# A four-stage hybrid block on one core: inverse sums as column-tile products, folds one step sooner, sine products on GpSimd, and first weights of the second attention split ahead

## The reference, cut to what matters

```python
x = x + _L0_attn_a_ref(_layernorm(x), q_a_w, q_b_w, kv_a_w, kv_b_w, o_w)
x = x + _L0_ffn_ref(_layernorm(x), Wg, Wu, Wd, Wr, temperature)
x = x + _L0_attn_b_ref(_layernorm(x), wq, wk, wv, wo)
x = x + _L0_ffn_ref(_layernorm(x), Wg, Wu, Wd, Wr, temperature)
# attention A, per head: softmax(query @ key.T) @ v, then @ o_w.T
attn = jax.nn.softmax(scores.astype(jnp.float32), axis=-1)
out = jnp.einsum('bhqk,bhkd->bhqd', attn, v)
```

## Time and profile before

| what | value |
|---|---|
| median of 3 runs | 1576.9 us |
| lowest and highest run | 1568.78 and 1577.12 us |
| profiled execution, its own time | 1568.78 us |
| its span, first to last instruction | 1567.0 us |
| instructions in the trace | 26377 |
| mean granted clock of TensorE | 0.979 of full speed |

### The profile page before, as it was taken

One profiled execution on the slowest core, in us unless ns is written; L12 is line 12 of the kernel. 1 busy time (PEld: TensorE's weight loads), 2 busy tenths in 40 slices (PEclk: granted clock), 3 DMA queues, 4 the chain that ended last, 5 costly groups with the idle time before them and its releaser, 6 DMA issues. The chain is left out here.

```text
span 1567.0 us, 26377 instructions
## 1 busy us (share of the span) xinstructions
PE 1464.7 (93%) x8888; PEld 1261.7 (81%) x8888; DVE 1174.5 (75%) x2637; ACT 849.3 (54%) x2068; POOL 630.4 (40%) x509
## 2 busy tenths in 40 slices
PE   5599999999699999997999999999999979999998
PEld 4477777777588888885799999999999868888887
DVE  6688898898775555567888888888888777555554
ACT  3688888887333332323767666666666523333332
POOL 2578888886200000004666666666666400000000
PEclk9799999999899999998999999999999989999999
DMA  2055445544400010001322222222231200001001
GB/s 98 17 124 123 109 116 123 117 108 107 123 21 21 21 41 0 1 1 41 88 67 63 68 56 73 61 68 68 43 87 41 61 21 20 21 22 40 0 1 54
DMA packets 47542, 91.52 MB, mean 58 GB/s; under 512 B 5184, under 2 KB 25664, under 8 KB 47424
## 3 DMA queue, kind: packets, MB, share of 16 engines
q1 hardware_dynamic: 47424, 90.01, 22.7%
HBM read 29.18 MB, written 2.10 MB: 20 GB/s over the span
## 5 line engine op out<-in xcount | busy, mean ns | idle before, releaser
L1722 DVE TENSOR_TENSOR f_hidden<-ps,f_silu 128x512 f32<-128x512 f32 x128 | 87.7, 690 | 201.9 <-PE ps L116 201.9
L1612 ACT ACTIVATE f_silu<-ps 128x512 f32<-128x512 f32 x128 | 76.3, 598 | 282.4 <-PE ps L116 282.4
L387 POOL TENSOR_TENSOR ab_swapped<-ab_swapped,const 128x512 f32<-128x512 f32 x124 | 160.2, 1292 | 169.6 <-ACT ab_swapped L382 169.6
L114 PE MATMUL ps<-xh,f_wl 128*128 128x512 f32 x512 | 203.2, 397 | 1.5 <-DVE f_hidden L1722 1.5
L115 PE MATMUL ps<-xl,f_wh 128*128 128x512 f32 x512 | 202.8, 396 | 0.0
L116 PE MATMUL ps<-xh,f_wh 128*128 128x512 f32 x512 | 202.6, 396 | 0.0
L1438 POOL TENSOR_TENSOR ab_qk<-ab_qk,ab_swapped 128x512 f32<-128x512 f32 x124 | 170.0, 1371 | 9.7
L73 POOL TENSOR_TENSOR rstd<-shifted,minus_half 128x4 f32<-128x4 f32 x16 | 16.5, 1032 | 364.7 <-DVE shifted L67 361.5
L1195 ACT ACTIVATE ab_probs<-ab_probs,ab_negmax 128x128 f32<-128x128 f32 (+1 forms) x256 | 114.7, 449 | 81.4 <-DVE ab_negmax L1299 79.4
L114 PE MATMUL ps<-f_wh,f_hl 128*128 128x256 f32 x512 | 144.4, 282 | 3.3 <-DVE x L1738 3.3
L115 PE MATMUL ps<-f_wl,f_hh 128*128 128x256 f32 x512 | 143.9, 281 | 0.0
(11 more groups left out here) (200 smaller groups left out, 4431.8 us busy)
## 6 DMA issues: line engine op xcount, KB each, us to landing
ab_probsT<-ab_squares SPq DMA_DIRECT2D x128, 192.0 KB, 3.7
aa_probsT<-f_stages SPq DMA_DIRECT2D x64, 256.0 KB, 4.5
b_stages<-keys SPq DMA_DIRECT2D x64, 256.0 KB, 4.7
f_stages<-wf_in SPq DMA_DIRECT2D x16, 768.0 KB, 4.3
b_stages<-wb_qkv_in SPq DMA_DIRECT2D x8, 768.0 KB, 6.4
a_stage<-wa_in SPq DMA_DIRECT2D x8, 608.0 KB, 5.9
x<-x_in SPq DMA_DIRECT2D x4, 512.0 KB, 7.4
b_stages<-wb_out_in SPq DMA_DIRECT2D x8, 256.0 KB, 3.8
```

Of the source, the lines that this page charges most:

```text
L114: nc.tensor.matmul(out, ll, rh, start=start, stop=False)
L387: return engine.tensor_tensor(by_batch(out), by_batch(src), table(c, rows, col), ALU.mult)
L1722: nc.vector.tensor_tensor(hidden[:, m, :], UP(m), silu[:, m, :], ALU.mult).then_inc(hid_done, 1)
```

## The change: what it does

1. `turn_inverse` reads the inverse sums themselves, broadcast as 64 equal weight columns, and multiplies them with the identity: eight plain fp32 products into column tiles in place of four transposes of 128x128. `widen` on POOL is gone, and the inverse sums have two buffers.
2. In step 3 PE issues `output`, then `turn_inverse`, then both halves of the mix, and the scores of step 3 behind them. Before, the first half stood in step 2 and the scores of step 3 ahead of the output.
3. `fold_query` and `fold_output` move on PE from the middle of step 2 to the end of step 1, and write bank `INVERSE` in place of `PROJ(0)`. On ACT and DVE they move from step 3 to step 2. Since `turn_inverse` writes the same bank, it waits for `fold_lo` or `wo_lo` in those slots.
4. The sine product of h = 0 moves from DVE to POOL, where that of h = 1 already is.
5. The first weights of attention B are split in the last expert's s = 1, and its first four projections stand behind the last expert's last product, ahead of `norm_turn` of group 1.

```diff
             def turn_inverse(n):
-                pe.wait_ge(wide_done, n + 1)
+                it, s = at(n)
+                pe.wait_ge(inv_done, n + 1)
                 after(pe, spread_done, n)
+                if fold_after(n):
+                    pe.wait_ge(fold_lo, fold_after(n))
+                if s == 1 and it + 1 < HP:
+                    pe.wait_ge(wo_lo, it + 2)
                 for t in range(TG):
-                    ins = nc.tensor.transpose(INVERSE[:, t * P:(t + 1) * P], wide[:, t].rearrange("p h d -> p (h d)"), c.ident)
+                    for h in range(2):
+                        ins = nc.tensor.matmul(INVERSE[64 * h:64 * h + 64, t * P:(t + 1) * P], inv[:, n % 2, t, h:h + 1].to_broadcast([P, KVR]), c.ident, start=True, stop=True)
                 ins.then_inc(inverse_ready, 1)
...
             def step(n, j):
-                if exists(n, j, LEAD):
+                if j < 3 and exists(n, j, LEAD):
                     scores(*pair_at(n, j, LEAD))
...
-                if j == 2 and fold_after(n):
-                    fold_query(fold_after(n), min(n + 3, SLOTS - 1))
-                if j == 2 and s == 1 and it + 1 < HP:
-                    pe.wait_ge(rope_read, 2 * (n + 3) + 1)
-                    pe.wait_ge(swap_done, 2 * (n + 3) + 1)
-                    fold_output(it + 1, PROJ(0))
-                if j >= 2:
-                    mix(n, j - 2)
+                if j == 1 and fold_after(n):
+                    fold_query(fold_after(n), n)
+                if j == 1 and s == 1 and it + 1 < HP:
+                    pe.wait_ge(spread_done, n)
+                    fold_output(it + 1, INVERSE)
                 if j == 3:
                     turn_inverse(n)
+                    mix(n, 0)
+                    mix(n, 1)
+                    if exists(n, j, LEAD):
+                        scores(*pair_at(n, j, LEAD))
...
-                if j == 3 and fold_after(n):
+                if j == 2 and fold_after(n):
                     fold_query(fold_after(n))
-                if j == 3 and s == 1 and it + 1 < HP:
-                    fold_output(it + 1, PROJ(0))
+                if j == 2 and s == 1 and it + 1 < HP:
+                    fold_output(it + 1, INVERSE)
...
-                if j == 1 and n + 3 < SLOTS:
-                    sines(n + 3, 0)
...
-            def widen(n):
-                pool.wait_ge(inv_done, n + 1)
-                after(pool, inverse_ready, n)
-                nc.gpsimd.tensor_copy(wide[:], inv[:].unsqueeze(3).to_broadcast([P, TG, 2, KVR])).then_inc(wide_done, 1)
...
+def first_weights_b(nc, b):
+    def upper(act):
+        act.wait_ge(b.stage_in, 16)
+        for part in PARTS_B:
+            nc.scalar.copy(flat_b(b.wh[:, 0, part]), flat_b(b.stage[:, part])).then_inc(b.w_hi, 1)
+        act.wait_ge(b.wo_in, 16)
+        nc.scalar.copy(b.woh[:, 0], b.wo_stage[:]).then_inc(b.wo_hi, 1)
...
+def first_projections_b(nc, c, b, pe, norm):
+    pe.wait_ge(b.w_lo, 1)
+    pe.wait_ge(norm.lo_done, KD)
+    for i, bank in enumerate(first_banks_b(c)):
+        col = slice((i // 2) * P, (i // 2) * P + P)
+        for k in range(KD):
+            ins = matmul3(nc, bank, (b.wh[:, 0, i % 2, k, col], b.wl[:, 0, i % 2, k, col]), (c.xh[:, k, 0:G], c.xl[:, k, 0:G]), k == 0, k == KD - 1)
+        ins.then_inc(b.proj_ready, 1)
...
                         down(it, e, s, first and e == 0 and s == 0)
+                        if last and e == 1 and s == 3 and b:
+                            pe.wait_ge(hid_done, 2 * NG * E)
+                            first_projections_b(nc, c, b, pe, norm)
```

More of the change, by code:

```diff
@@ L489, in _, with fold_query @@
         def _(pe):
-            def fold_query(it, last_projected):
+            def fold_query(it, n):
                 pe.wait_ge(stage_in, 16 * (it + 1))
-                if last_projected is not None:
-                    pe.wait_ge(rope_read, 2 * last_projected + 1)
-                    pe.wait_ge(swap_done, 2 * last_projected + 1)
+                after(pe, spread_done, n)
                 fold_product(nc, FOLD(it)[:, 0:P], stage, 0).then_inc(fold_ready, 1)
@@ L512, in project @@
                     after(pe, fold_rest, it)
[L513 to L518, removed]
                 free = 0 if n < 2 else h + 1 if n == 2 else 2 * n + h - 1
@@ L814, in step @@
                     invert(n + 1)
-                if j == 3 and fold_after(n):
+                if j == 2 and fold_after(n):
                     fold_query(fold_after(n))
-                if j == 3 and s == 1 and not last:
-                    fold_output(it + 1, PROJ(0))
+                if j == 2 and s == 1 and not last:
+                    fold_output(it + 1, INVERSE)
                 if last and s >= 2 and j == 2:
@@ L925, in _ @@
             for n in range(SLOTS):
-                widen(n)
                 if n >= 1:
@@ L941, in _, with flat_b, first_banks_b, lower @@
                 norm_rstd(nc, c, norm, pool, s)
-def attention_b(nc, c, name, w_qkv, w_out, stage, wo_stage, stage_in, wo_in, own_norm, norm, ahead):
+PARTS_B = [slice(0, 2), slice(2, 3)]
+def flat_b(w):
+    return w.rearrange("p a k d -> p (a k d)")
+def first_banks_b(c):
+    return [c.ps[:, bank, :] for bank in (0, 1, 3, 2)]
+def first_weights_b(nc, b):
[5 more added lines that the diff above has]
+        nc.scalar.copy(b.woh[:, 0], b.wo_stage[:]).then_inc(b.wo_hi, 1)
+    def lower(dve):
+        for i, part in enumerate(PARTS_B):
+            dve.wait_ge(b.w_hi, i + 1)
+            nc.vector.tensor_tensor(flat_b(b.wl[:, 0, part]), flat_b(b.stage[:, part]), flat_b(b.wh[:, 0, part]).bitcast(F32), ALU.subtract).then_inc(b.w_lo, 1)
+        dve.wait_ge(b.wo_hi, 1)
+        nc.vector.tensor_tensor(b.wol[:, 0], b.wo_stage[:], b.woh[:, 0].bitcast(F32), ALU.subtract).then_inc(b.wo_lo, 1)
+    return upper, lower
+def first_projections_b(nc, c, b, pe, norm):
[6 more added lines that the diff above has]
+        ins.then_inc(b.proj_ready, 1)
+def attention_b(nc, c, name, b, w_qkv, w_out, stage, wo_stage, stage_in, wo_in, own_norm, norm, ahead):
     W, SQ, LEAD = T + P, 32, 7
@@ L975, in attention_b @@
         VALUES = c.ps[:, 2, :]
-        FIRST = [c.ps[:, bank, :] for bank in (3, 4, 5, 2)]
+        FIRST = first_banks_b(c)
         MIX = lambda h: c.ps[:, 5 + h, :]
@@ L1032, in project @@
                 for k in range(KD):
-                    ins = matmul3(nc, FIRST[i] if n == 0 else PROJ(i), (wh[:, half, i % 2, k, col], wl[:, half, i % 2, k, col]), (c.xh[:, k, g], c.xl[:, k, g]), k == 0, k == KD - 1)
+                    ins = matmul3(nc, PROJ(i), (wh[:, half, i % 2, k, col], wl[:, half, i % 2, k, col]), (c.xh[:, k, g], c.xl[:, k, g]), k == 0, k == KD - 1)
                 ins.then_inc(proj_ready, 1)
@@ L1129, in head_pair @@
                         step(it, half, s, j)
-            for i in range(4):
-                project(0, 0, 0, i)
             norm_turn(nc, c, own_norm, pe, 2, own_banks)
@@ L1443, in _, with experts @@
                 norm_rstd(nc, c, norm, pool, s)
-def experts(nc, c, name, weights, stage, stage_in, own_norm, ahead=(), norm=None, result=None):
+def experts(nc, c, name, weights, stage, stage_in, own_norm, ahead=(), norm=None, result=None, b=None):
     with ExitStack() as ctx:
@@ L1630, in turn @@
                             split_hi(*((it, 1) if e == 0 else (it + 1, 0)))
+                        if s == 1 and last and e == 1 and b:
+                            first_weights_b(nc, b)[0](act)
                         if last and e == 1 and s == 2 and norm:
@@ L1759, in turn @@
                             split_lo(*((it, 1) if e == 0 else (it + 1, 0)))
+                        if s == 1 and last and e == 1 and b:
+                            first_weights_b(nc, b)[1](dve)
                         if last and e == 1 and s == 2 and norm:
@@ L1826, in hybrid_kernel @@
             attention_a(nc, c, "aa", a, wa, a_stage, a_in, norm2, [(f_stage[:, e], wf[e], f1_in[e]) for e in range(2)])
-        experts(nc, c, "f1", wf, f_stage, f1_in, norm2, ahead=[(b_stage[:], wb_qkv[0], b_in), (bo_stage[:], wb_out[0], bo_in)], norm=norm3)
-        attention_b(nc, c, "ab", wb_qkv, wb_out, b_stage, bo_stage, b_in, bo_in, norm3, norm4, [(f_stage[:, e], wf[e], f2_in[e]) for e in range(2)])
+        with ExitStack() as inner:
+            sb, sem = lambda n, s, d=F32: inner.enter_context(nc.sbuf_tensor(n, s, d)), lambda n: inner.enter_context(nc.semaphore(f"ab_{n}"))
+            b = Core()
+            b.wh, b.wl = sb("b_wh", [P, 2, 3, KD, 2 * P], F32R), sb("b_wl", [P, 2, 3, KD, 2 * P], F32R)
+            b.woh, b.wol = sb("b_woh", [P, 2, 2, D], F32R), sb("b_wol", [P, 2, 2, D], F32R)
+            b.w_hi, b.w_lo, b.wo_hi, b.wo_lo, b.proj_ready = sem("w_hi"), sem("w_lo"), sem("wo_hi"), sem("wo_lo"), sem("proj_ready")
+            b.stage, b.wo_stage, b.stage_in, b.wo_in = b_stage, bo_stage, b_in, bo_in
```

(2 more changed lines are left out.)

40 lines of the change are left out of this document (14 added, 26 removed).

## The result

| | before | after |
|---|---|---|
| median | 1576.9 us (4 runs) | 1640.6 us (4 runs, 1639.35 to 1644.94) |
| span of the profiled execution | 1567.0 us | 1639.4 us |
| mean granted clock | 0.979 | 0.966 |

The ratio of after to before is 1.0426, with a 95% interval from 1.0407 to 1.0446. The forecast was 1613 us, from 1583 to 1640: slower was right, the size was not. The measured loss is 64 us by medians and 72 us between the profiled executions.

What follows compares the result with a forecast made beforehand. PE was taken to bound attention A, DVE close behind. Slots 1 to 28 at 320.8 us against 290.7 gave +30, the clock +10: 1609 from the profiled 1568.8; 4 us for scatter made 1613 us, range 1583 to 1640.

Steps and rivals of the forecast that it cites:

- The new order makes a chain: Attention A, plain slots: output waits 0.6 us for `mixed_lo`, ready at 6.6 us; the slot ends at 10.1 us.
- the 13 waits of L549: Attention A, `turn_inverse`: expected to wait for the folds' splits 13 times, about 2.4 us each.
- outputs that wait for `aa_ml`: Attention A: PE's output products were expected to wait for POOL's low half of the mix, 0.6 us in plain slots.
- Fold slots: Attention A: query-fold slots end at 13.4 us with a 2.4 us stall, output-fold slots at 12.7 with 2.5.
- The clock: Attention A: half speed behind half of the 13 fold stalls, at 1.5 us each, +10 us, between 0 and 22.
- The last slots: End of attention A, slots without projections: left as they are, 0, at most +3 us.
- The price of the inverse products: `turn_inverse` on PE: eight plain products take 0.86 us against 0.41 for the transposes, +0.45 us.
- Sines at no cost: Sine product moved to POOL: 9.7 us of POOL work with dispatch, in slots of 10.1 and more; no cost.
- The border at 0: Experts to attention B: projections fill 2.1 us of idle but push `norm_turn` back; gain 0, between -2 and +2 us.
- Dearer: Rival, 12 in 100: every stall followed by half clock, +22 for +10, or products take twice: 1625 to 1645 us.

## Why the prediction was wrong in size

That the kernel gets slower was right, and so was the kind of cause: the new order opens a chain through DVE, ACT and POOL, and the folds stall `turn_inverse`. Which link of the chain ends last was wrong, and with it the size. The median lies 0.6 us above the end of the range. Against the profiled execution the prediction's sum was 1609, measured 1641.2: 32 us short.

- **The step that failed is "The new order makes a chain".** It lets the output wait 0.6 us for `mixed_lo`, and ends the slot at 10.1 us. `mixed_lo` came at 6.61 of 6.6. But the output has a second condition, `out_added`, and the walk left out DVE's items between the normalisation and that addition: two ropes, a row maximum, squares. The output starts at 7.66, behind a wait of 1.49. The slot's rest was 3.63 against 3.55, so the slot took 11.3 us. Over 15 plain slots these 1.2 us are 18 us. The experiment with the additions early shows the cause: the wait goes, and a plain slot takes 10.3 to 10.6. Of the signs that the prediction named, the 13 waits of L549 came, 1.9 to 2.9 us each; outputs that wait for `aa_ml` came only in the first and the last slots.
- **Fold slots** were 13.3 against 12.7 and 13.8 against 13.4, together 7 x 0.6 + 6 x 0.4 = 6.6 us. The folds' own wait was 1.9 and 2.4 us where 2.5 and 2.4 were walked. In the slots of the output fold PE had waited before that at the output, for the same addition: 0.73 us in five of them, 1.08 at 203.14. In those of the query fold it had not; there PE itself came to the stall 0.4 us later than walked (8.6 for 8.2).
- **The clock** was sized nearly right: 8 falls of 1.7 us are 13, against the 10 put down. That about half of the stalls would be followed by a fall was a guess, and that it was close is luck as far as the runs show: they don't tell the 8 from the other 5. That this is the clock is read from the granted clock in the windows and from slot lengths; no experiment held the order and changed the clock alone, so its exact share stays open.
- **The last slots** were left at 0, "at most +3", and cost 6.1. Between 448 and 478 us the outputs wait 4.5 us for `aa_ml` and the mean clock is 0.83. Slots without projections have no work between the scores and the output, so the chain stands bare. This is read from the trace, not tried.
- These make 18 + 6.6 + 3.4 + 6.1 = 34 us; the start of the program gave back 2.6, and two output-fold slots took 14.0 and 13.6 us in place of 13.3. The medians lie closer (27.6 us short), since 4 us were added for the scatter of the runs before, and the profiled execution after lies 0.6 above its median.
- **The price of the inverse products was right**: 206.00 to 206.89 is 0.89 us, against 0.86. By the Trainium skill, "TensorE: Matmul & The Clock Gate", section Terms, the transpose mode is 4 times faster for fp32, and the estimate from that was some 1.7; this trace disagrees, and the measurement decides. Alone they cost no time: PE is busy 259.15 us of the stretch there in place of 250.41, and its 7.7 us of waiting for the folds at L525 are gone. Why the folds come in time there was not followed up.
- **Sines at no cost** held: 0.9981 alone, with POOL at 244 of 260 us.
- **The border at 0** held nearly: alone it measured 2.6 us less, where -2 to +2 was given. The experts' last product ends and the first rope of attention B follows 10.4 us later, both before (702.9 to 713.34 in the earlier trace rows) and after, as the timeline there shows:

```profile
776.78 0.39 PE L114 MATMUL ps<-xh,b_wl 128*128 128x512 f32 x1
...
782.40 1.04 PE L92 MATMUL ps<-const,normed 128*128 128x128 f32 x8
...
787.19 0.68 DVE L387 TENSOR_TENSOR ab_qk<-ps,const 128x512 f32<-128x512 f32 x1
```

Four projections now take 5.6 us there, of which PE was idle for 2.1, and `norm_turn` moves back by the other 3.5, as predicted. Where the 2.6 us come from is not shown.

The rival *Dearer* named half clock behind every stall, or products of twice the price; neither came. Its time, 1625 to 1645, was met by another way.

The prediction blamed the wait for `mixed_lo` and the folds. The experiments put it more simply. The scores of step 3 feed DVE and ACT; issued behind the output, the inverse and both mixes, they leave DVE without work for 3 to 5.6 us behind every mix, and everything that PE later needs from DVE, the addition and the splits of the folds, comes late by it. The place of the scores costs 48 to 53 us in the changed kernel, the sooner folds 17 to 21. All the other parts together give back 4 us, and 7 if the mix stays in two runs.

## What to carry to other kernels

Walk a chain with every semaphore of the waiting instruction, the one that frees its output bank too, and with every instruction that stands ahead of each releaser on its in-order engine; the latest arrival counts, not the one that the change is about. On the bounding engine, issue what feeds the other engines ahead of a long run that only it works on: here that was worth 48 to 53 us in the changed kernel, and the merged run of column tiles nothing that could be measured. A wait removed alone came back at the next semaphore three times here (folds back, additions early, one run of tiles), and moving the sines, neutral alone, shortens DVE's chain once that chain holds PE. So time edits in pairs too before judging one.

## What the runs showed of the hardware

- Plain fp32 products of 128 columns into two column tiles take 0.89 us for 16 passes, 0.11 us a pair. Per 128x128 block that is 0.22 us, about twice the transposes' 0.10 in the earlier trace rows.
- The granted clock fell to half (0.50, 1.2 GHz) behind stretches that were only in part idle: PE had been busy 0.97 of the 3.40 us before. It did so behind 8 of 13 such stalls of 1.9 to 2.9 us, and stayed at 1.00 behind the other 5, with PE busy 0.95 of 3.40 us before one of them. A fall cost 1.7 us more in the slot behind it.
